# Gated cross-attention and routed experts: output projection as three fp32r products, and a new order of work in the tiles

## Chip, cores, metric

The kernel runs on one core of one Trainium2 chip. The metric is the device time of one launch in microseconds (us); the numbers below are medians of several launches. The engines of the core are TensorE (in the profile PE, its weight loads PEld), VectorE (DVE), ScalarE (ACT), GpSimd (POOL) and SyncE (SP, here only a DMA queue). Each works through its own instructions in the order in which they are written, and waits at semaphores for the others.

## What is computed

The reference, cut to what matters (2 x 1024 tokens of 256 numbers, 16 heads of 16, 77 context rows per batch, 8 experts with 1024 hidden units, of which each token takes the one with the largest router probability):

```
x = x + tanh(g_xattn) * attention(layernorm(x), ctx)      # Q, K, V, softmax over 77 keys, out @ wo.T + bo
x = x + tanh(g_ffn) * experts(layernorm(x))               # router = softmax(xt @ Wr + br)
# experts: h = relu(xn @ W1[idx] + b1[idx]); y = (h @ W2[idx] + b2[idx]) * gate
```

All inputs and the output are float32. The part that the change touches is `out @ wo.T` and what stands around it.

## The kernel before

The 2048 rows are cut into NT = 16 tiles of 128 rows. The launch has three stages: a start (weights transposed, K and V of the context prepared), the tile stage (attention, residual, layer norm and router for each tile; each tile's rows, their normalized form and their gate are stored to a scratch array in memory), and the expert stage (slots of 128 rows that share an expert are gathered from the scratch array, go through the two expert layers and are scattered to the output).

In the tile stage the loop `for n in range(NT)` stands once in the block of each engine, and round n of it mixes work on several tiles, written out by hand:

- TensorE in round n: `scores(n)` into pS; `transpose_O(n-2)`, which transposes the attention output On into the two halves of bank pA; `transpose_P(n-1, 0)`; `project(n-2)`, the output projection of tile n-2 into bank pB; the rest of the transposes of the probabilities of tile n-1 and of the next x (the latter into pA); `attend(n-1)`, the probabilities times V, into pB again; `query(n+1)`; `route(n)`, the router's product.
- ScalarE in round n: `copy_OT(n-2)` (pA into the SBUF tile OT, the stationary operand of the projection), `copy_PT(n-1, 0)`, `exp(n, 0)`, `copy_PT(n-1, 1)`, `copy_XX(n+1)`, `copy_PT(n-1, 2)`, `exp(n, 1)`, `query(n+1)` (the two copies of Q with its bias), `z_row(n-3)` and `x2_row(n-2)` (they write the row to be stored into one of three buffers `pay`; before tile i's they wait that the store of row i-3 has landed), `gate_exp(n-3)`.
- VectorE in round n: `smax(n, 0)` (row maxima of half the scores), `ssub(n, 0)` (their subtraction), `resid(n-2)` (projection in pB plus x; it frees pB for `attend(n-1)`), `smax(n, 1)`, `ssub(n, 1)`, layer norm statistics of two tiles, the router of tile n-3, the normalized x of tile n+2, and `norm(n-1)` in three steps (clamp of the softmax denominators into rden, reciprocal, product into On). Small steps of generators (`next(...)`) stand between the large ones.
- GpSimd in round n: `rstd2(n-2)` and `rstd1(n+3)` (powers for the layer norms), x plus bias, `store_row(n-4)` (the DMA to the scratch array), in some rounds steps of an expert-bias split.
- SyncE's queue: the weights of the last three experts (6, 7, 5) go into areas that the tile stage has used; each of these six loads of 1 MB is started when `x2_row` has counted one tile further (act_px2).

After round 15 follows a tail, written out for the tiles y = 14 and z = 15: on TensorE `transpose_O`, `project` and `attend` for them with the counts and ranks of the router between them, on VectorE the tables for the first slots (`rank`, `first_table`, `first_slots`), the first gather indices idxg and scatter indices idxs, `resid(y)`, `norm(z)`, `resid(z)`. Then the first slot begins with `transpose_z(0)` (again into pA) and `hidden(0, 0)`.

The projection of a tile is two matmuls in float32, one for each half of the 256 rows of the weight `wT["wo"]` (tile woT, 264 columns: 256 outputs and 8 router columns), at line 1647. In a trace each float32 matmul has two records. `OT` is written by ScalarE at line 623 and `xs` by VectorE at line 940. A float32 matmul by another way stands already in the expert stage: the second layer splits its hidden values and its weights in a high part rounded to fp32r and a low part, the rest, and adds three fp32r products (lines 1925 and 1930).

## Time and profile before

| | us |
|---|---|
| median of 3 runs | 278.69 |
| lowest, highest | 278.66, 279.93 |
| the profiled execution | 280.71 |
| its span in the trace | 278.8 |
| TensorE busy in it (matmuls) | 270.6 |
| VectorE, ScalarE, GpSimd busy | 202.9, 166.2, 135.8 |

The profile is of one execution. Its span runs from the first instruction to the last; the launch takes 1.9 us more than that. Times in the trace are counted from the start of the span. The tile stage lies between about 18 and 137 us, the expert stage behind it. A row of the trace that says `[0.17 <-DVE On L933]` means that the engine stood idle for 0.17 us before it, and that VectorE's instruction of line 933, which writes On, released it.

### The profile page before, as it was taken

Reading aid. Unit: us, or ns where it says so; the run is one execution under the profiler, and the core shown is the slowest. Engines: PE = TensorE matmul, PEld = TensorE weight load, DVE = VectorE, ACT = ScalarE, POOL = GpSimd, SP = SyncE. Lnnn points to the kernel's source line nnn. Section 1 sums busy time; section 2 is a strip of 40 time slices with the busy share of each in tenths; the row PEclk is TensorE's granted clock in tenths of the full one; section 3 lists DMA queues with packets and bytes.
Section 4 is the critical chain, followed back from the end, with each engine's and each line's share of the span. In section 5 each row is a group of like instructions: output and inputs, shape, how many; then the busy total and the mean of one; then the engine's idle time right before and its main releaser. Section 6 shows DMA issues by size and latency. Waiting matters only on the chain.

```text
span 278.8 us, 7269 instructions
## 1 busy us (share of the span) xinstructions
PE 270.6 (97%) x2320; PEld 239.7 (86%) x2320; DVE 202.9 (73%) x687; ACT 166.2 (60%) x444; POOL 135.8 (49%) x259
## 2 busy tenths in 40 slices
PE   8999999999999999999999999999999999999993
PEld 4879899999899999997888989999878789988992
DVE  6698579888888888879869976995446537443564
ACT  2535467777677777776396665785438435453551
POOL 3444046777877778644778242642212242222422
PEclk9999799999999999999999999999999999999999
DMA  7999996000002464545323131412201111220212
GB/s 206 288 307 374 372 378 243 33 36 31 30 29 89 186 185 182 183 175 185 117 76 118 58 99 57 136 46 75 77 9 59 52 51 49 83 58 24 60 49 72
DMA packets 19693, 34.43 MB, mean 124 GB/s; under 512 B 2392, under 2 KB 14486, under 8 KB 19643
## 3 DMA queue, kind: packets, MB, share of 16 engines
q1 hardware_dynamic: 15369, 21.26, 23.1%
q0 software_dynamic: 4128, 12.49, 13.7%
q8 instruction: 25, 0.41, 0.6%
q14 instruction: 25, 0.20, 0.2%
q10 hardware_dynamic: 146, 0.07, 0.1%
HBM read 27.45 MB, written 6.75 MB: 123 GB/s over the span
## 4 chain that ended last, share of the span: by engine, by line
PE 87%; DVE 6%; DMA 4%; issue 2%; POOL 0%; DVEq 0%; ACT 0%; POOLq 0%
PE pS L1855 21%; PE pB L1629 12%; PE pB L1925 10%; PE pT L1542 7%; PE pB L1647 6%; PE pA L1542 5%; PE pB L1930 5%; PE pS L1585 4%; PE pA L1565 3%; PE pT L1565 3%; DMA zin<-rows_dram,idxg 3%; PE pT L1657 2%; DMA W2s<-in_ctx_dram 1%; DVE hA L1304 1%; PE pT L1880 1%
## 5 line engine op out<-in xcount | busy, mean ns | idle before, releaser
L1855 PE MATMUL pS<-znf,W1c 128*128 128x128 f32 x576 | 71.2, 277 | 0.2 <-issue 0.2
L1855 PEld LDWEIGHTS pS<-znf,W1c 128*128 128x128 f32 x576 | 67.1, 192 | 3.4 <-issue 2.9
L458 POOL DMA_INDIRECT out_dram<-yo,idxs x17 | 17.4, 1021 | 73.0 <-DVE yo L1335 61.9
L1629 PE MATMUL pB<-VB,PT 128*128 128x51 f32 (+1 forms) x320 | 39.0, 270 | 0.2 <-DVE xs L940 0.2
L1925 PE MATMUL pB<-W2p,hT 128*128 128x512 f32 x136 | 39.0, 408 | 0.0
L745 ACT ACTIVATE hA<-pS,b1s 128x128 f32<-128x128 f32 x72 | 20.5, 367 | 30.6 <-PE pS L1855 27.7
L1629 PEld LDWEIGHTS pB<-VB,PT 128*128 128x128 f32 (+1 forms) x320 | 38.1, 192 | 0.6 <-issue 0.6
L1304 DVE TENSOR_SCALAR hA<-pS,b1s 128x128 f32<-128x128 f32 x72 | 20.2, 342 | 18.6 <-PE pS L1855 15.2
L605 ACT ACTIVATE Pb<-Pb 128x616 f32<-128x616 f32 x32 | 23.0, 718 | 15.4 <-DVE Pb L914 15.4
L756 ACT ACTIVATE hT<-hA 128x512 fp32r<-128x512 f32 x36 | 23.0, 641 | 15.2 <-DVE hA L1304 15.1
L441 POOL DMA_INDIRECT zin<-rows_dram,idxg x21 | 22.7, 1082 | 11.4 <-issue 5.3
L1925 PEld LDWEIGHTS pB<-W2p,hT 128*128 128x128 f32 x136 | 23.0, 189 | 4.8 <-issue 1.7
L906 DVE TENSOR_REDUCE mx<-pS 128x8 f32<-128x616 f32 x32 | 25.3, 790 | 1.9 <-PE pS L1589 1.9
L914 DVE TENSOR_TENSOR Pb<-pS,mx 128x616 f32<-128x616 f32 x32 | 25.3, 792 | 1.0
L1542 PE MATMUL pT<-cst,Pb 128*128 128x128 f32 (+1 forms) x160 | 25.5, 277 | 0.0
L1311 DVE TENSOR_TENSOR hT<-hA,hT 128x512 fp32r<-128x512 f32 x36 | 24.3, 686 | 1.5 <-ACT hT L756 0.2
L1930 PEld LDWEIGHTS pB<-W2p,hT 128*128 128x128 f32 x136 | 20.7, 188 | 3.9 <-DVE hT L1311 0.8
L613 ACT ACTIVATE PT<-pT 128x512 f32<-128x512 f32 x32 | 19.0, 595 | 7.2 <-PE pT L1542 6.5
L1930 PE MATMUL pB<-W2p,hT 128*128 128x256 f32 x136 | 21.5, 280 | 0.4 <-DVE hT L1311 0.4
L1542 PEld LDWEIGHTS pT<-cst,Pb 128*128 128x128 f32 (+1 forms) x160 | 19.5, 142 | 2.2 <-issue 0.5
L1647 PE MATMUL pB<-woT,OT 128*128 128x264 f32 x64 | 19.3, 426 | 0.6
L395 POOL TENSOR_SCALAR mv<-mv 128x1 f32<-128x1 f32 x16 | 3.8, 236 | 27.6 <-DVE mv L949 27.4
(279 smaller groups left out, 531.0 us busy)
## 6 DMA issues: line engine op xcount, KB each, us to landing
W1s<-in_L_ffn_W_dram SPq DMA_DIRECT2D x8, 1024.0 KB, 10.2
W2s<-in_L_ffn_W_dram SPq DMA_DIRECT2D x8, 1024.0 KB, 11.2
rows_dram<-pay POOLq DMA_DIRECT2D x16, 260.0 KB, 2.6
xs<-in_x_dram SPq DMA_DIRECT2D x3, 512.0 KB, 5.8
W2s<-in_sel_dram SPq DMA_DIRECT2D x1, 385.0 KB
zin<-rows_dram,idxg POOLq DMA_INDIRECT x21, 3.7
out_dram<-yo,idxs POOLq DMA_INDIRECT x17
W1s<-in_L_xattn_wk_dram SPq DMA_DIRECT2D x1, 256.0 KB, 3.1
```

Of the source, the lines that this page charges most:

```text
L605: e.activation(p2, p2, ACT.Exp, scale=0.25).then_inc(g["act_P"], 1)
L756: e.activation(hT[s % 2][0][:, 512 * n:512 * n + 512], half_of(s, n)[:, :], ACT.Copy).then_inc(g["act_hT"], 1)
L906: e.tensor_reduce(mx[:, i % 2, 8 * m:8 * m + 8].rearrange("p (n h) -> p n h", n=2), heads(m), AX.X, ALU.max).then_inc(g["dve_own"], 1)
L914: e.tensor_tensor(Pb[i % 2][:, 616 * m:616 * m + 616].rearrange("p (n h k) -> p n h k", n=2, h=4), heads(m), mx[:, i % 2, 8 * m:8 * m + 8] ...
L1304: e.tensor_scalar(half_of(s, 1)[:, 128 * c:128 * c + 128], pS[:, 2 * (s % 2) + 1, 128 * c:128 * c + 128], b1s[:, 4 + c, s:s + 1], 0.0, ALU ...
L1311: e.tensor_tensor(lo, half_of(s, n)[:, :], hi, ALU.subtract).then_inc(g["dve_hT"], 1)
L1542: return e.transpose(o, i, ident[0:n, 0:n])
L1629: t = e.matmul(pB[:, 17 * h0:17 * h0 + 51], PT[i % 2][0:n, c, :], VB[0:n, b, c, :], start=(c == 0), stop=(c == NC - 1), skip_group_check=True)
L1647: t = e.matmul(pB[:, 0:DX], OT[:, k, :], wT["wo"][:, k, :], start=(k == 0), stop=(k == 1))
L1855: t = e.matmul(pS[:, 2 * (s % 2) + n, 128 * c:128 * c + 128], W1c[k][n][:, 128 * c:128 * c + 128], znf[s % 2][:, 128 * k:128 * k + 128], s ...
L1925: e.matmul(o2, hT[s % 2][0][:, 128 * c:128 * c + 128], W2p[c // 2][:, :, D * (c % 2):D * (c % 2) + D], start=False, stop=True, skip_group_ ...
L1930: t = e.matmul(o, hT[s % 2][1][:, 128 * c:128 * c + 128], W2p[c // 2][:, 0, D * (c % 2):D * (c % 2) + D], start=False, stop=True, skip_gro ...
```

## The change

The projection's operands are split. ScalarE writes OT as fp32r (the rounded, high part); VectorE writes a new tile OT_low, pA minus OT, in `low_O(i)`. The weight is split once, in round 1 and 2: `wo_parts[:, 0]` by a copy on ScalarE, `wo_parts[:, 1]` by the subtraction `wo_low()` on VectorE. `project(i)` is then six fp32r matmuls: OT with both weight parts (four), then, after a wait for VectorE, OT_low with the high weight part (two). All that waited for OT to be copied because it wanted to write pA again now waits for VectorE's `dve_OT`.

In the tiles VectorE does `low_O` and `resid` ahead of `ssub(n, 0)`, with the first step of the next x's statistics between them. ScalarE's `exp(n, 0)` goes from between two `copy_PT` to where `exp(n, 1)` stood, `x2_row` and `z_row` come right behind it and ahead of `query(n+1)`, and `exp(n, 1)` comes last. Some tiles change their place in SBUF. One counter of semaphores (dve_idg2) is merged into another to make room for the new one.

```
-                exp(n, 0)
+                if n < 2:
+                    exp(n, 0)
...
-                    exp(n, 1)
+                    exp(n, 1 if n == 1 else 0)
+                if n == 2:
+                    e.wait_ge(g["dve_pois"], 1)
+                if n >= 2:
+                    x2_row(n - 2)
+                if n >= 3:
+                    z_row(n - 3)
...
                 if n >= 3:
-                    z_row(n - 3)
-                if n == 2:
-                    e.wait_ge(g["dve_pois"], 1)
+                    gate_exp(n - 3)
                 if n >= 2:
-                    x2_row(n - 2)
-                if n >= 3:
-                    gate_exp(n - 3)
+                    exp(n, 1)
...
+                    e.wait_ge(g["act_wT"], 5)
+                    e.activation(wo_parts[:, 0, :, :], wT["wo"][:, :, :], ACT.Copy).then_inc(g["act_wT"], 1)
...
+            def wo_low():
+                e.wait_ge(g["act_wT"], 7)
+                e.tensor_tensor(wo_parts[:, 1, :, :], wT["wo"][:, :, :], wo_parts[:, 0, :, :], ALU.subtract).then_inc(
+                    g["dve_wrc"], 1)
+
+            def low_O(i):
+                e.wait_ge(g["act_OT"], i + 1)
+                if i:
+                    e.wait_ge(g["pe_pr"], i)
+                e.tensor_tensor(OT_low[:, :, :].rearrange("p k n -> p (k n)"), pA[:, 0:256],
+                                OT[:, :, :].rearrange("p k n -> p (k n)"), ALU.subtract).then_inc(g["dve_OT"], 1)
...
+                if n == 2:
+                    wo_low()
+                if n >= 2:
+                    low_O(n - 2)
+                    next(x_stats, None)
+                    next(gated_row, None)
+                    resid(n - 2)
                 ssub(n, 0, t)
-                next(gated_row, None)
-                if n >= 2:
-                    resid(n - 2)
...
+            low_O(y)
             resid(y)
...
+            low_O(z)
             resid(z)
...
                 if i == 0:
-                    e.wait_ge(g["act_wT"], 5)
+                    e.wait_ge(g["dve_wrc"], 3)
+                for part in range(2):
+                    for k in range(2):
+                        e.matmul(pB[:, 0:DX], OT[:, k, :], wo_parts[:, part, k, :], start=(part == 0 and k == 0),
+                                 stop=False)
+                e.wait_ge(g["dve_OT"], i + 1)
                 for k in range(2):
-                    t = e.matmul(pB[:, 0:DX], OT[:, k, :], wT["wo"][:, k, :], start=(k == 0), stop=(k == 1))
+                    t = e.matmul(pB[:, 0:DX], OT_low[:, k, :], wo_parts[:, 0, k, :], start=False, stop=(k == 1))
```

The order that this gives. On VectorE, a round of the tile stage (from the first smax, line 906 before and 914 after, to the second ssub, 914 before and 922 after), first before, then after:

```order
109 L906 TENSOR_REDUCE mx<-pS 128x8
110 L991 RECIPROCAL Lg<-Lg 128x1
111 L914 TENSOR_TENSOR Pb<-pS,mx 128x616
112 L997 TENSOR_SCALAR pay<-Lg,tg 128x1
113 L940 TENSOR_TENSOR xs<-pB,xs 128x264
114 L906 TENSOR_REDUCE mx<-pS 128x8
115 L945 BN_STATS st<-xs 128x6
116 L914 TENSOR_TENSOR Pb<-pS,mx 128x616
117 L874 BN_STATS st<-xs 128x6
```

The same round after:

```order
135 L914 TENSOR_REDUCE mx<-pS 128x8
136 L1011 RECIPROCAL Lg<-Lg 128x1
137 L953 TENSOR_TENSOR OT_low<-pA,OT 128x256
138 L882 BN_STATS st<-xs 128x6
139 L1017 TENSOR_SCALAR pay<-Lg,tg 128x1
140 L960 TENSOR_TENSOR xs<-pB,xs 128x264
141 L922 TENSOR_TENSOR Pb<-pS,mx 128x616
142 L914 TENSOR_REDUCE mx<-pS 128x8
143 L965 BN_STATS st<-xs 128x6
144 L922 TENSOR_TENSOR Pb<-pS,mx 128x616
```

The new subtraction stands behind the first smax, the residual ahead of both ssub (Pb), and one of the statistics is drawn in between them.

On ScalarE, a round from `copy_OT` to the last instruction ahead of the next one, before:

```order
67 L623 ACTIVATE OT<-pA 128x256
68 L613 ACTIVATE PT<-pT 128x512
69 L605 ACTIVATE Pb<-Pb 128x616
70 L613 ACTIVATE PT<-pT 128x512
71 L586 ACTIVATE XX<-pA 128x256
72 L616 ACTIVATE PT<-pT 128x128
73 L617 ACTIVATE PT<-pT 80x128
74 L605 ACTIVATE Pb<-Pb 128x616
75 L599 ACTIVATE QT<-pA,bcol 128x128
76 L599 ACTIVATE QT<-pT,bcol 128x128
77 L641 ACTIVATE pay<-xs,mv 128x256
78 L634 ACTIVATE pay<-xs,pois 128x256
```

The same round after:

```order
66 L616 ACTIVATE PT<-pT 128x512 x2
67 L589 ACTIVATE XX<-pA 128x256
68 L619 ACTIVATE PT<-pT 128x128
69 L620 ACTIVATE PT<-pT 80x128
70 L608 ACTIVATE Pb<-Pb 128x616
71 L637 ACTIVATE pay<-xs,pois 128x256
72 L644 ACTIVATE pay<-xs,mv 128x256
73 L602 ACTIVATE QT<-pA,bcol 128x128
74 L602 ACTIVATE QT<-pT,bcol 128x128
75 L649 ACTIVATE Lg<-Lg 128x8
76 L608 ACTIVATE Pb<-Pb 128x616
```

Both row copies (pay) now stand ahead of both Q copies (QT), and the second exponential (Pb) stands last, right ahead of the next `copy_OT`.

In the tail, on VectorE, what stands behind the scatter indices idxs of the first slots, before:

```order
412 L1389 TENSOR_TENSOR idxs<-xh 128x4
413 L940 TENSOR_TENSOR xs<-pB,xs 128x264
```

and after:

```order
428 L1414 TENSOR_TENSOR idxs<-xh 128x4
429 L953 TENSOR_TENSOR OT_low<-pA,OT 128x256
```

The subtraction that the last projection waits for has the residual's old place, behind the tables and the routers.

## Rows read from the trace of the kernel before

**Rows 1.** Windows: stretch, length, busy us (count) of PE, PEld, DVE, ACT, POOL, clock, DMA share, GB/s.

```profile
88.23:95.32 7.09, 7.05 (x70) 6.44 (x67) 6.21 (x23) 5.37 (x15) 5.58 (x14) 1.00 0.46 187
31.00:32.00 1.00, 1.00 (x5) 0.79 (x4) 0.63 (x1) 0.69 (x2) 0.00 (x0) 0.50 1.01 395
```

**Rows 2.** Timeline, round 10: start, duration, engine, line, what, count, idle before.

```profile
88.36 0.79 DVE L906 TENSOR_REDUCE mx<-pS 128x8 f32<-128x616 f32 x1
...
88.70 0.38 ACT L623 ACTIVATE OT<-pA 128x256 f32<-128x256 f32 x1 [0.46 <-PE pA L1542]
...
89.14 1.16 PE L1647 MATMUL pB<-woT,OT 128*128 128x264 f32 x4
...
90.13 0.60 PE L1542 MATMUL pT<-cst,Pb 128*128 128x128 f32 x4
90.33 0.43 DVE L940 TENSOR_TENSOR xs<-pB,xs 128x264 f32<-128x264 f32 x1 [0.15 <-PE pB L1647]
...
93.89 0.37 ACT L599 ACTIVATE QT<-pT,bcol 128x128 f32<-128x128 f32 x1
...
94.27 0.17 DVE L923 TENSOR_SCALAR rden<-pB 128x16 f32<-128x16 f32 x1 [0.65 <-PE pB L1629]
...
94.57 0.81 PE L1585 MATMUL pS<-Kbd,QT 32*128 32x154 f32 x16
...
95.32 0.20 PEld L1542 LDWEIGHTS pA<-cst,On 128*128 128x128 f32 x2 [0.17 <-DVE On L933]
```

**Rows 3.** Timeline of PE in the expert stage: the products with fp32r operands.

```profile
187.62 0.63 PE L1930 MATMUL pB<-W2p,hT 128*128 128x256 f32 x4
188.09 1.09 PE L1925 MATMUL pB<-W2p,hT 128*128 128x512 f32 x4
```

**Rows 4.** Timeline, round 2; last, a page group: shape, count | busy us, mean ns | idle.

```profile
29.94 0.79 DVE L906 TENSOR_REDUCE mx<-pS 128x8 f32<-128x616 f32 x1
...
31.07 1.96 PE L1647 MATMUL pB<-woT,OT 128*128 128x264 f32 x4
...
L1311 DVE TENSOR_TENSOR hT<-hA,hT 128x512 fp32r<-128x512 f32 x36 | 24.3, 686 | 1.5 <-ACT hT L756 0.2
```

**Rows 5.** Timeline of DVE: round 3, and the last round, 15.

```profile
44.11 0.17 DVE L923 TENSOR_SCALAR rden<-pB 128x16 f32<-128x16 f32 x1
...
125.00 0.79 DVE L906 TENSOR_REDUCE mx<-pS 128x8 f32<-128x616 f32 x1
...
126.96 0.79 DVE L906 TENSOR_REDUCE mx<-pS 128x8 f32<-128x616 f32 x1
...
129.63 0.17 DVE L923 TENSOR_SCALAR rden<-pB 128x16 f32<-128x16 f32 x1 [0.26 <-PE pB L1629]
```

**Rows 6.** Timeline of the tail: residual of tile 14; projection and residual of tile 15.

```profile
132.79 0.43 DVE L940 TENSOR_TENSOR xs<-pB,xs 128x264 f32<-128x264 f32 x1 [0.42 <-PE pB L1647]
...
138.24 1.16 PE L1647 MATMUL pB<-woT,OT 128*128 128x264 f32 x4
...
140.29 0.16 DVE L1389 TENSOR_TENSOR idxs<-xh 128x4 int32<-128x4 f32 x1
140.40 0.43 DVE L940 TENSOR_TENSOR xs<-pB,xs 128x264 f32<-128x264 f32 x1
```

**Rows 7.** Timeline of the expert stage's start: the first gather that PE waits for.

```profile
159.78 1.01 POOL L441 DMA_INDIRECT zin<-rows_dram,idxg  x1 [2.77 <-DVE idxg L1484]
...
163.55 0.44 PE L1542 MATMUL pA<-cst,zin 128*128 128x128 f32 x2 [0.45 <-DMA zin<-rows_dram,idxg]
```

**Rows 8.** Round 9 and 10: a row's store, its time to landing, the row copy, a weight load.

```profile
88.14 0.37 SPq L321 DMA_DIRECT2D W1s<-in_L_ffn_W_dram  x1
89.95 0.65 POOL L422 DMA_DIRECT2D rows_dram<-pay  x1
DMA to landing us min/median/max: 4.3/4.3/4.3
94.64 0.49 ACT L634 ACTIVATE pay<-xs,pois 128x256 f32<-128x256 f32 x1
```

More of the change, by code:

```diff
@@ L112, in flamingo @@
         VB = sbt("VB", [128, B, NC, 51])
-        woT = sbt("woT", [128, 2, DX])
+        wo_parts = sbt("wo_parts", [128, 2, 2, DX], F32R)
+        OT_low = sbt("OT_low", [128, 2, 128], F32R)
         On = sbt("On", [128, D])
-        OT = sbt("OT", [128, 2, 128])
+        OT = sbt("OT", [128, 2, 128], F32R)
         mx = sbt("mx", [128, 2, H])
         rden = sbt("rden", [128, 2, H])
-        Pb1 = sbt("Pb1", [128, NC * 128])
+        sbt("below_PT1", [128, 496])
         PT1 = sbt("PT1", [128, NC, 128])
@@ L129, in flamingo @@
         st = sbt("st", [128, 4, 8])
-        sbt("below_W1c", [128, 2124])
+        Pb1 = sbt("Pb1", [128, NC * 128])
+        woT = sbt("woT", [128, 2, DX])
+        sbt("below_W1c", [128, 316])
         Pb = [sbt("Pb0", [128, NC * 128]), Pb1]
@@ L565, in _ @@
             used = e.value_load(slot_e[0:1, NS:NS + 1], min_val=FIRST, max_val=NS)
-            e.wait_ge(g["dve_idg2"], 1)
+            e.wait_ge(g["dve_ids2"], 2)
             for grp in range(2):
                 gather_small(grp)
-            e.wait_ge(g["dve_ids2"], 2)
+            e.wait_ge(g["dve_ids2"], 3)
             for s in range(KA - 1, FIRST):
@@ L1506, in _ @@
             e.wait_ge(g["dve_own"], t)
[L1507 removed]
+            e.tensor_tensor(idxg[:, NS:NS + 2], idt2, ids2[:, 0, :], ALU.add).then_inc(g["dve_ids2"], 1)
             e.wait_ge(g["dve_own"], t_e)
@@ L1637, in transpose_O @@
                 if i == NT - 1:
-                    e.wait_ge(g["act_OT"], NT - 1)
+                    e.wait_ge(g["dve_OT"], NT - 1)
                 transpose(pA[:, 0:128], On[:, 0:128])
@@ L1756, in _ @@
                     if n >= 2:
-                        e.wait_ge(g["act_OT"], n - 1)
+                        e.wait_ge(g["dve_OT"], n - 1)
                     else:
@@ L1862, in transpose_small_z @@
                 if grp == 0:
-                    e.wait_ge(g["dve_ids2"], 2)
+                    e.wait_ge(g["dve_ids2"], 3)
                     e.wait_ge(g["dve_b1"], 2)
```

5 lines of the change are left out of this document (2 added, 3 removed).

## The prediction

> **What bounds the kernel now.** I read the windows first, then the timeline of one round, then the rounds that differ from it. In a middle round TensorE is busy for 7.05 of 7.09 us [rows 1]; VectorE works 6.21 and ScalarE 5.37. The timeline of that round [rows 2] shows where TensorE still waits: its weight load for the projection starts 0.06 us after ScalarE has written OT (88.70 + 0.38 = 89.08, then 89.14), and its next transposes of On wait 0.17 us for VectorE (95.32). VectorE waits twice: 0.15 us for the projection ahead of the residual (90.33) and 0.65 us for attend ahead of rden (94.27). So TensorE sets the pace, but a loop through VectorE (attend, rden, On, transposes) lies right under it: whatever comes late to On is paid in full. The question is what the projection gives back per round, and where VectorE's new instruction stands in a wait of TensorE.
>
> **Part 1, the projection in a round.** Before: from the weight load at 89.14 the first matmul starts some 0.1 later (one load), and the next transposes start at 90.13 [rows 2]. That is four records of (90.13 - 89.24) / 4 = 0.222 us, 0.89 in all; a record is two passes of 264 columns at 0.111. After: six fp32r products. The expert stage shows their price: four of 256 columns take 188.09 - 187.62 = 0.47, so 0.117 each [rows 3], and 0.12 for 264 columns. The first four run from 89.24 to 89.72. The last two wait for OT_low. Its price is not in the trace. Nearest is the residual, 264 columns from PSUM and SBUF, 0.43 us [rows 2]; the fp32r subtraction of 512 columns in SBUF takes 0.69 [rows 4], half of that is 0.34. I take 0.42, with 0.34 to 0.5 as ends. It starts when smax is through (88.36 + 0.79 = 89.15) and OT is written (89.08), ends at 89.58, the weight load behind it starts at 89.64, and the matmuls at 89.75: two of them, until 89.99. That is 0.14 less than 90.13; with the ends 0.06 to 0.17. I take 0.12.
>
> The trace prices two passes at 0.222. The Trainium skill, "FP8 and Floating Point Precision", section Matmul Precision, says that true FP32 takes four passes through the array, while reduced FP32 reads the number once and truncates it; by that rule alone eight passes become six, and each round would give back 0.22, not 0.12. The rows agree with the count of passes; the difference is the weight load and the wait for OT_low, which the rule leaves out.
>
> **Part 2, VectorE's round.** It gets one instruction more (0.36 from start to start, as the residual has it: such instructions overlap by some 0.07), and part of it lies in the wait for the projection. Counted through: OT_low 89.15, statistics 89.50, gate 89.84, residual 90.21 (last product 89.87, plus 0.28 to its end as in [rows 3], where 0.63 is three steps of 0.117 and the last one's 0.28; plus 0.06 for the semaphore), first ssub 90.57, second smax 91.28, second ssub 92.3, and the rest of the round as before: VectorE is ready for rden at about 93.85. attend is through 0.12 earlier than before, at 94.15. So 0.3 us of the 0.65 are left, and the round holds at -0.12.
>
> Round 3 is another matter. There rden starts at 44.11 with no wait in front [rows 5], because the mask of the second batch is made in it. Counted the same way VectorE comes to rden at 44.37. TensorE would be ready for it at 43.98. So this round is 0.26 slower than before.
>
> **Part 3, ScalarE's round.** The two row copies (0.49 for the one at 94.64 [rows 8], the other somewhat longer) go ahead of the Q copies. The first exponential can start at about 91.8 and end at 92.45; the row copy from 92.4, the Q copies at 93.5 and 93.8; the second one ended at 93.89 + 0.37 = 94.26 before and scores started at 94.57 [rows 2]. There is room for about 0.4. It is used up by a wait that was hidden before: the row copy needs the landing of the store three rows back. A store issued at 89.95 landed 4.3 later, at 94.25, just ahead of the copy at 94.64 [rows 8]. That store was slow because a weight load of 1 MB had started at 88.14, let go by the row copy of the round before. With the copy 2 us earlier the load goes 2 us earlier too and is nearly over when the store is issued; I take 2.4 to 3 us to landing (an estimate between the 4.3 of this row and none of the load beside it). The store itself goes about 0.35 later (the statistics that GpSimd waits for are later). So the row copy starts at about 92.7 to 93.0 and scores at 94.3 to 94.6: no loss in rounds without a load, and most of the 0.12 gone in the rounds with one. I count rounds 4 to 9 with -0.12 (six, -0.7) and rounds 10 to 14 with -0.04 (five, -0.2).
>
> **Part 4, the first projection.** The split of the weight comes once. ScalarE's copy is hidden (it ends before OT(0)). VectorE's subtraction (528 columns, 0.69 as for 512 [rows 4]) starts behind smax, at 30.7, and OT_low behind it. Before, the four records ran from 31.07 [rows 4] at half clock (0.50 in that stretch [rows 1]), so at 0.44 each, until 32.83. After: weight load 31.4, four products of 0.22 from 31.6, two more, end 32.95. I count +0.15, with -0.1 to +0.6.
>
> **Part 5, the last round and the tail.** Here OT_low stands where VectorE is late already.
> - Round 15: VectorE starts its first smax at 125.00, behind steps of the router's ranks; the second smax is at 126.96, and rden at 129.63 after a wait of 0.26 [rows 5]. After: OT_low 125.71 to 126.13, products end 126.70, residual 126.76, ssub 127.11, second smax 127.82. That is 0.86 later, less the 0.26: On comes 0.6 later. TensorE waits for it. +0.6.
> - Tile 14: the residual at 132.79 waited 0.42 for the projection [rows 6], that is, tables kept VectorE until 132.37. OT_low(14) starts there, ends 132.79; two products, and the residual at 133.35. +0.55, also for TensorE, whose transposes stand behind the project.
> - Tile 15: TensorE starts the projection at 138.24, and VectorE has its residual at 140.40, right behind idxs at 140.29 [rows 6]. OT_low(15) takes that place: 140.40 to 140.83, products from 141.0, residual 141.46. VectorE is 1.06 later; TensorE, whose first slot starts behind the projection, 2.0. What of this is carried on? The first gather that TensorE waits for (0.45 at 163.55) was issued at 159.78, when VectorE had its indices [rows 7]. That chain is VectorE's and moves by 1.06, and TensorE's extra 0.9 goes into this wait and one at the first slot. +1.06.
>
> **The sum.** +0.15 + 0.26 - 0.7 - 0.2 + 0.6 + 0.55 + 1.06 = +1.7 us. Against the span: 278.8 to 280.5, and the profiled execution 280.71 (1.9 around the span) to 282.4. That execution lies 2.0 above the median of the runs, 278.69; the difference applied to the median gives 280.4.
>
> **Rivals.**
> - *All of the passes are won.* If OT_low is ready when the fourth product ends, a round gives 0.17 to 0.22: twelve rounds -2.3. For it: VectorE has slack in the rounds. Against: the count in part 1. With the other terms +2.6 it comes to 279.0, not slower than before. It decides if OT_low is done before 89.6 on the clock of round 10. The skill's count of passes would lead here.
> - *The row copy waits for its store.* If stores still take 4.3 us, the copy starts at 94.6, ScalarE's Q copies some 1.6 later than now, and scores 1.5 late once in two rounds: 0.6 a round, in rounds 10 to 14 +3, in all 283.4. For it: [rows 8]. Against: the load that made the store slow moves with the copy. It decides from 3 us to landing on.
> - *The clock stays low, or falls again.* It is at half, 1.2 GHz, in round 2, in a stretch where TensorE was busy throughout [rows 1], so it can be low without an idle engine. After the change TensorE stands idle for 0.5 us there, and for 2 us at tile 15. For it: these gaps. Against: rounds with gaps of 0.1 to 0.2 us ran at 1.00 [rows 1]. A further stretch of 3 us at half clock does work of 1.6 us less: 280.4 + 1.6 = 282.0. It decides if the granted clock is 0.5 past 33 or past 139.
> - *Faster.* Full gain of 0.22 in twelve rounds (-2.6), and the tail's delays (2.2) fully absorbed by gathers: 278.69 - 2.6 + 0.4 = 276.5. It needs that VectorE's chain of the tail is not what the gather waits for; [rows 7] names just that.
>
> **How the numbers follow.** A measurement of this kernel can tell about 0.5% from no change, 1.4 us: faster is under 277.3, slower over 280.1. Forecast as summed 0.48, all passes won 0.18, row copy 0.13, clock 0.12, faster 0.09. About a third of the forecast's own spread (279.6 to 281.2, from the ends of the price of OT_low and of part 4) lies below 280.1. Slower: 0.32 + 0.13 + 0.12 = 0.57; same: 0.16 + 0.18 = 0.34; faster 0.09. The likeliest is 280.4. The range 278.2 to 283.0 leaves out most of the faster case and the upper part of the row copy's.
>
> **What would show it.** In a middle round, project to next transposes 0.85 instead of 0.99 us, and a round of 6.98; VectorE's wait at rden about 0.3. In round 3 TensorE waits for On 0.5. Behind tile 15's fourth product about 2 us of idle time on TensorE, released by OT_low. Wrong would be: rounds of 7.1 or more with ScalarE waiting for a store; half clock behind 139; or a gather at 163.55 that has not moved.

## The result and the profile after

The changed kernel is slower. Its four executions took 284.34, 285.95, 287.63 and 288.63 us, median 286.79; beside them the kernel before took 278.77 (278.66 to 279.93). The ratio is 1.0218, interval 1.0128 to 1.0307. In a later set of runs it was 286.76 against 280.5: 1.0179, interval 1.0130 to 1.0227. Both intervals are clear of 1; both hold 1.02, so whether it is more than 2% is open. Ratios and intervals, here and below, leave out executions more than 1.5% above the fastest of their kernel; the medians do not. The forecast was 280.4, with a range up to 283.0. The sign was right, the size was not.

Two engines' lines of the page of after, the granted clock in 40 slices, and the chain that ended last:

```profile
PE 270.2 (96%) x2352; PEld 241.5 (85%) x2352; DVE 208.1 (74%) x704; ACT 164.6 (58%) x445; POOL 135.8 (48%) x259
...
PEclk9999799999999999999889999999999999999999
...
PE 69%; DVE 14%; issue 5%; DMA 5%; POOL 3%; ACT 3%; ACTq 0%; DVEq 0%; POOLq 0%
...
PE pS L1886 19%; PE pB L1956 10%; PE pB L1655 7%; PE pT L1568 5%; PE pB L1961 5%; PE pA L1568 4%; PE pB L1674 3%; DVE Pb L922 3%; PE pS L1611 3%; DMA rows_dram<-pay 2%; PE pA L1591 2%; PE pB L1678 2%; DVE mx L914 2%; PE pT L1591 2%; DMA zin<-rows_dram,idxg 1%
```

The store of a row (DMA rows_dram<-pay) holds 2% of the chain, and the clock has a second dip in the middle of the span. The profiled execution is the fastest of the four (284.34, span 282.5, against 278.8 before), so its trace explains 3.7 us; the other three have lower mean clocks (0.974 to 0.980, against 0.988), and I come to them below.

**A steady round does what was forecast.** TensorE in round 9, and the scores of round 10; timeline (start, duration, engine, line, what, idle before):

```profile
82.40 0.75 PE L1674 MATMUL pB<-wo_parts,OT 128*128 128x264 f32 x4
82.99 0.41 PE L1678 MATMUL pB<-wo_parts,OT_low 128*128 128x264 f32 x2
83.24 0.60 PE L1568 MATMUL pT<-cst,Pb 128*128 128x128 f32 x4
...
87.17 0.57 PE L1688 MATMUL pT<-wrc,XX 128*128 128x8 f32 x4
89.08 0.81 PE L1611 MATMUL pS<-Kbd,QT 32*128 32x154 f32 x16 [1.33 <-ACT QT L602]
```

From projection to next transposes it is 83.24 - 82.40 = 0.84 us; in [rows 2] it was 0.99. But at 89.08 the scores wait 1.33 us for QT. ScalarE shows why, and the second and third line show how long the store issued at 83.61 took to land:

```profile
87.52 0.51 ACT L637 ACTIVATE pay<-xs,pois 128x256 f32<-128x256 f32 x1 [1.85 <-DMA rows_dram<-pay]
...
L425 POOL DMA_DIRECT2D rows_dram<-pay x1: 662/662/662, 83.6 to 83.6; - x1
...
DMA to landing us min/median/max: 3.8/3.8/3.8
```

The row copy waits 1.85 us for its store, and both Q copies stand behind it. The windows of that time (columns as in [rows 1]) show that no load was beside it:

```profile
84.50:85.00 0.50, 0.50 (x7) 0.50 (x6) 0.50 (x2) 0.50 (x4) 0.41 (x2) 1.00 0.47 158
85.00:85.50 0.50, 0.50 (x7) 0.50 (x6) 0.50 (x2) 0.50 (x2) 0.48 (x1) 1.00 0.93 366
85.50:86.00 0.50, 0.50 (x6) 0.50 (x6) 0.50 (x2) 0.17 (x1) 0.40 (x1) 1.00 0.04 8
86.00:86.50 0.50, 0.50 (x6) 0.50 (x6) 0.50 (x4) 0.00 (x0) 0.00 (x0) 1.00 0.06 17
...
88.12 0.37 SPq L324 DMA_DIRECT2D W1s<-in_L_ffn_W_dram  x1
```

Most of the store moved by 85.7, at up to 366 GB/s; it landed at 83.61 + 3.8 = 87.4, and the weight load was issued only at 88.12, by the copy that had waited.

The trace also shows what held the landing up. Between its issue and its landing one packet of another queue moved; of the queues from 82 to 88 us (packets, MB, share of the engines' time), the first is the store's:

```profile
q0 software_dynamic: 80, 0.27, 11.6%
q8 instruction: 1, 0.02, 1.2%
```

The queue that the profile calls "instruction" moved 16 KB from 84.93 to 86.10, in the middle of the store. The store is 64 packets of 4 KB and 16 of 4 bytes, so four and one for each of the 16 DMA engines. Sixty of the 64 were through at 85.7; the last four, one engine's share, started one after another from 86.10 on, as soon as the 16 KB were through, and ended at 86.9. All 18 traces, of before, after and e1 to e16, agree. They record 118 landings of row stores that had no weight load beside them. All twenty of 3 us or more had such a 16 KB packet that began 0.8 to 2.0 us after the issue, and none that had no packet of an instruction queue took over 2.5. In the kernel before this packet moved at 85.70, behind the store of 82.86, which landed in 2.4. This is read from traces; no run moved that packet alone.

**The clock falls a second time.** The first stretch at half clock is that of [rows 1]; the second was not there before:

```profile
31.00:32.00 1.00, 0.57 (x4) 0.20 (x2) 1.00 (x3) 0.53 (x2) 0.00 (x0) 0.50 0.98 361
...
139.00:140.00 1.00, 1.00 (x35) 0.83 (x32) 0.79 (x4) 0.00 (x0) 0.76 (x1) 0.77 0.25 96
140.00:141.00 1.00, 1.00 (x4) 0.42 (x3) 0.93 (x9) 0.00 (x0) 0.76 (x3) 0.50 0.04 8
141.00:142.00 1.00, 1.00 (x5) 0.47 (x3) 0.86 (x5) 0.38 (x1) 0.99 (x2) 0.50 0.82 250
142.00:143.00 1.00, 1.00 (x6) 0.94 (x4) 0.89 (x6) 0.22 (x2) 0.74 (x3) 0.52 0.07 25
```

**The places where VectorE is late.** The first projection, the ends of rounds 3 and 15, the two tiles of the tail, and the gather of [rows 7]:

```profile
31.95 1.22 PE L1674 MATMUL pB<-wo_parts,OT 128*128 128x264 f32 x4 [0.43 <-DVE wo_parts L946]
...
46.13 0.20 PEld L1568 LDWEIGHTS pA<-cst,On 128*128 128x128 f32 x2 [0.61 <-DVE On L941]
...
133.16 0.20 PEld L1568 LDWEIGHTS pA<-cst,On 128*128 128x128 f32 x2 [0.69 <-DVE On L941]
...
135.20 0.52 PE L1678 MATMUL pB<-wo_parts,OT_low 128*128 128x264 f32 x2 [0.36 <-DVE OT_low L953]
...
143.33 0.42 DVE L953 TENSOR_TENSOR OT_low<-pA,OT 128x256 fp32r<-128x256 f32 x1
143.81 0.51 PE L1678 MATMUL pB<-wo_parts,OT_low 128*128 128x264 f32 x2 [0.59 <-DVE OT_low L953]
...
167.01 0.44 PE L1568 MATMUL pA<-cst,zin 128*128 128x128 f32 x2 [0.49 <-DMA zin<-rows_dram,idxg]
```

The gather has moved from 163.55 [rows 7] to 167.01, 3.46 us, which is nearly all of the 3.7.

### The profile page after: what moved, and what is told of

The parts are those of the page before. It is cut to its first block, busy times and chain, and to the rows that moved or that the text cites. A ratio compares the mean times of both kernels' runs of the same rounds, so it can differ in the third digit from the quotient of the medians.

```text
span 282.5 us, 7366 instructions
## 1 busy us (share of the span) xinstructions
PE 270.2 (96%) x2352; PEld 241.5 (85%) x2352; DVE 208.1 (74%) x704; ACT 164.6 (58%) x445; POOL 135.8 (48%) x259
## 4 chain that ended last, share of the span: by engine, by line
PE 69%; DVE 14%; issue 5%; DMA 5%; POOL 3%; ACT 3%; ACTq 0%; DVEq 0%; POOLq 0%
PE pS L1886 19%; PE pB L1956 10%; PE pB L1655 7%; PE pT L1568 5%; PE pB L1961 5%; PE pA L1568 4%; PE pB L1674 3%; DVE Pb L922 3%; PE pS L1611 3%; DMA rows_dram<-pay 2%; PE pA L1591 2%; PE pB L1678 2%; DVE mx L914 2%; PE pT L1591 2%; DMA zin<-rows_dram,idxg 1%
## 5 line engine op out<-in xcount | busy, mean ns | idle before, releaser
L731 ACT ACTIVATE znf<-pA,bcol 128x128 f32<-128x128 f32 x38 | 15.6, 476 | 0.8 <-PE pA L1568 0.8
```

## The experiments

All are medians of the executions of one set, with the ratio to the kernel before in the same set. "Clock" is the median of the executions' mean granted clock. "Less clock" is the median of time minus (1 - clock) x span, that is, the time with the half-clock stretches counted at half of their length. It is only a guide: where TensorE waits for something else, a slow stretch costs less than that (e15 and e16 below differ by 0.7 us in their medians, and this measure puts 1.9 of theirs on the clock).

| kernel | n | median us | ratio (95%) | clock | less clock |
|---|---|---|---|---|---|
| before (four sets) | 19, 27, 29, 35 | 280.5, 280.2, 280.5, 281.1 | 1 | 0.993 | 278.4 to 278.9 |
| changed | 4 | 286.79 | 1.0218 (1.0128 to 1.0307) | 0.977 | 280.6 |
| e12, changed again | 6 | 286.76 | 1.0179 (1.0130 to 1.0227) | 0.977 | 280.2 |
| e1, orders only | 10 | 282.73 | 1.0071 (1.0029 to 1.0113) | 0.989 | 279.2 |
| e2, products only | 10 | 281.0 | 1.0031 (0.9994 to 1.0068) | 0.985 | 277.3 |
| e3, ScalarE's old order | 4 | 294.41 | 1.0511 (1.0440 to 1.0582) | 0.980 | 288.9 |
| e4, OT_low early | 4 | 287.64 | none | 0.974 | 280.0 |
| e5, filled tail | 6 | 287.06 | 1.0230 (1.0190 to 1.0271) | 0.980 | 280.5 |
| e6, e2 + OT_low early | 12 | 280.13 | 0.9983 (0.9953 to 1.0013) | 0.994 | 276.9 |
| e7, x2 copy behind query | 9 | 282.94 | 1.0075 (1.0044 to 1.0106) | 0.984 | 278.3 |
| e8, e7 + OT_low early | 12 | 280.5 | 1.0020 (0.9990 to 1.0049) | 0.993 | 277.8 |
| e9, before, filled start | 12 | 279.89 | 0.9989 (0.9953 to 1.0024) | 0.999 | 279.7 |
| e10, e7 + filled tail | 14 | 283.37 | 1.0069 (1.0038 to 1.0101) | 0.988 | 279.9 |
| e11, e6 + wo in two steps | 12 | 279.69 | 0.9964 (0.9936 to 0.9992) | 0.988 | 276.9 |
| e13, e11 + filled start | 12 | 279.45 | 0.9957 (0.9921 to 0.9993) | 0.994 | 278.4 |
| e14, changed, all mends | 12 | 280.39 | 0.9985 (0.9951 to 1.0019) | 0.994 | 279.3 |
| e15, e9 + idle 2.3 us | 12 | 282.76 | 1.0059 (1.0019 to 1.0098) | 0.988 | 278.9 |
| e16, e9 + the same, filled | 12 | 282.02 | 1.0039 (1.0004 to 1.0075) | 0.996 | 280.1 |

### The parts of the change, one by one

e1 is the kernel before with both new orders and its own float32 projection:

```diff
 # VectorE, round n
-ssub(n, 0, t); next(gated_row, None)
-if n >= 2: resid(n - 2)
+if n >= 2: next(x_stats, None); next(gated_row, None); resid(n - 2)
+ssub(n, 0, t)
 # ScalarE: exp(n, 0), x2_row, z_row ahead of query(n + 1); exp(n, 1) behind it
```

> The kernel before with the new order alone (residual ahead of the first subtraction on VectorE, both exponentials and the two row copies in their new places on ScalarE); the projection is the float32 one. Two theories. Waits: of the 8 us of the change about 1.7 come from row copies that now wait for the store three rows back in the middle of ScalarE's round (1.2 + 0.3 + 0.15 us in rounds 9, 11 and 13), and this is their place: 280.5 to 281.5 us, with waits of ScalarE's row copy for the store again. Clock: most of the 8 us are further stretches at half clock (3.4 us long, 1.7 us of loss each), let loose by gaps of TensorE at the products' waits for OT_low; those are missing here, so the mean clock stays near that of before (0.994 or more), and this kernel is within 2 us of before. If the order itself lets the clock fall: 284 or more.

It was 0.7% slower. Its middle rounds are 7.09 us, those of before: the order alone gives nothing. The row copy waited up to 2.47 us for its store, with the float32 projection as well, and round 3 took 7.53 (7.10 before, 6.95 in e2 below). So these costs belong to the order, not to the products.

e2 has the products and neither order; low_O stands right behind the first smax:

```diff
 t = smax(n, 0)
+if n >= 2: low_O(n - 2)
 ssub(n, 0, t)
 next(gated_row, None)
 if n >= 2: resid(n - 2)
```

> The fp32r products alone, with both engines' order as before (OT_low right behind the first smax, subtraction, then residual). Waits: rounds at 6.98 instead of 7.09 us (-1.3 over twelve), first projection +0.7, round 3 +0.3, last round and tail +2.2, no wait of the row copies: 280.5 to 281. Clock: the gaps at the first projection and at tile 15 are still there, so the mean clock lies at 0.974 to 0.988 as in the changed kernel, and the time at 283 to 286.

Its middle rounds take 7.02 us, 0.07 less than before, and no row copy waits more than 0.5. The ratio, 1.0031, cannot be told from 1. Its clock is 0.985, and by the last column the gain goes there. The last projection of its tail:

```profile
139.51 0.51 PE L1675 MATMUL pB<-wo_parts,OT_low 128*128 128x264 f32 x2 [1.84 <-DVE OT_low L950]
...
141.00:142.00 1.00, 1.00 (x5) 0.55 (x3) 0.93 (x7) 1.00 (x4) 0.57 (x3) 0.50 0.78 166
```

TensorE waits 1.84 us for OT_low, and 1.5 us later the granted clock is 0.50.

e3 is the changed kernel with the ScalarE order of before:

> The changed kernel with ScalarE's order of before (exponential 0 between two copies, row copies behind Q's). Both theories: no wait of the row copy for its store, so rounds 9, 11 and 13 lose nothing: 1.7 us less than the changed kernel, 284.5 to 285.5, if the mean clock stays at 0.974 to 0.988. If the row copies' waits are what the clock hangs on, the clock comes back to 0.99 and the time to 281 or 282.

Every theory missed this. A round takes 7.90 us, 0.93 more than in the changed kernel. One round of e3, ScalarE and TensorE:

```profile
97.15 0.72 ACT L608 ACTIVATE Pb<-Pb 128x616 f32<-128x616 f32 x1 [1.61 <-DVE Pb L919]
97.77 0.58 ACT L616 ACTIVATE PT<-pT 128x512 f32<-128x512 f32 x1
...
98.40 1.09 PE L1652 MATMUL pB<-VB,PT 128*128 128x51 f32 x8 [0.76 <-ACT PT L616]
```

With the residual ahead of it, the first ssub is written 1 us later, ScalarE's exponential waits for it, and the second copy of PT, which TensorE needs for attend, stands behind that exponential. So the two orders belong together: whoever moves the residual forward on VectorE must move the exponential back on ScalarE.

### OT_low in the tail

e4 changes only the tail of the changed kernel, e6 makes the same edit on e2:

```diff
-together(islice(early, 5), islice(table, 5)); low_O(y)
+together(islice(early, 3), islice(table, 3)); low_O(y)
+together(islice(early, 2), islice(table, 2))
...
 together(router(y - 1))
+low_O(z)
...
-low_O(z)
 resid(z)
```

> The changed kernel with OT_low of tiles 14 and 15 made as soon as OT is there (in between the tables of tile 14, behind the router of tile 13), no other edit. Waits: TensorE's gaps of 0.6 us at tile 14 and 1.5 to 2 us at tile 15 go, VectorE's chain to the indices of the fifth slot is 0.5 + 0.6 us shorter: 285.5. Clock: with the gap behind tile 15 gone at least one half-clock stretch goes with it (1.7 us more): 283.5 or less, mean clock 0.98 or more in every run.

> The three products with both orders of before (as in e2), and in the tail the subtraction that makes OT_low ahead of the work that delayed it: for tile 14 after three pieces of the tables rather than five, for tile 15 ahead of the index arithmetic. In the profile of e2 project(15) waited 1.84 us and project(14) 0.41 us for it. Theory W: 2 us less than e2 when the clock is the same, so a time less the clock's share ((1 - mean clock) x span) of 274.5 to 275.5 against 276.6 in e2 and 278.5 before. Theory C adds: without the 1.84 us wait the stretch at half clock at 141 us goes in part of the executions, and the median is 276.5 to 278.5. If the wait only passes to the next item (gathered rows), 280 to 281.

Four executions of e4, from 282.38 to 292.01, settle nothing: its profile has row copies that wait 2.34 and 2.15 us, a stretch at half clock behind the second, and another from 140.2 on, in the tail, with no idle time of TensorE of 0.2 us or more in the 10 us ahead of it. On e2 the edit is clean. The last projection no longer waits, the window that stood at 0.50 in e2 is at 1.00, and the median clock goes from 0.985 to 0.994:

```profile
136.54 0.76 PE L1672 MATMUL pB<-wo_parts,OT 128*128 128x264 f32 x4
137.27 0.51 PE L1676 MATMUL pB<-wo_parts,OT_low 128*128 128x264 f32 x2
...
141.00:142.00 1.00, 0.88 (x8) 0.69 (x8) 0.95 (x6) 1.00 (x3) 1.00 (x2) 1.00 0.77 162
```

The ratio fell from 1.0031 to 0.9983 only, with intervals that overlap. Less the clock, the two are 277.3 and 276.9, not the 2 apart that I expected; the waits of 2.2 us that went were probably covered in part already.

### The row copy

e7 moves one instruction of the changed kernel; e8 has e4's edit too:

```diff
 if n >= 3: z_row(n - 3)
-if n >= 2: x2_row(n - 2)      # stood ahead of z_row
 if n + 1 < NT: query(n + 1)
+if n >= 2: x2_row(n - 2)
 if n >= 3: gate_exp(n - 3)
```

> The changed kernel, except that ScalarE copies a row's x part (x2_row, the copy that waits for the store of three tiles before) behind the evacuation of the next query and not ahead of it; z_row stays ahead. Theory W (the copy's wait for its store delays QT, the scores and the round: 1.2, 0.5 and 0.15 us in the rounds that end at 89.82, 104.17 and 118.96 us of the profile): all rounds 4 to 11 take 6.95 to 7.55 us and the time less the clock's share is 1.5 to 2 us under that of the changed kernel (280.6), so 278.7 to 279.1; the median about 283 to 285, as the clock decides. If the row copy's wait cost nothing by itself (the rounds were long for the clock or the scores' own inputs), the rounds stay at 8.3 and 7.4 us and the time at 286 to 287.

> The edits of e7 and the early OT_low in the tail (as in e4) together on the changed kernel. The sum of the parts, by waits: 280.6 less 1.8 (rows) less about 1 (OT_low at tiles 14 and 15) = 277.8 less the clock's share, which would be 279.5 to 282 on the clock of 0.994 to 0.985. Against e6 it tells whether the new order of both engines is worth its 0.08 us a round (6.95 against 7.02) once the row copy no longer waits: the new order costs 0.29 us in round 3 and the late OT wait of the first projection 0.5 us more, so e6 is expected to stay 1 to 3 us ahead.

```profile
86.64 0.37 ACT L602 ACTIVATE QT<-pT,bcol 128x128 f32<-128x128 f32 x1
87.50 0.51 ACT L637 ACTIVATE pay<-xs,pois 128x256 f32<-128x256 f32 x1 [0.49 <-DMA rows_dram<-pay]
...
87.33 0.81 PE L1611 MATMUL pS<-Kbd,QT 32*128 32x154 f32 x16
...
89.12 0.75 PE L1674 MATMUL pB<-wo_parts,OT 128*128 128x264 f32 x4 [0.18 <-ACT OT L626]
```

The store still lands late (4.2 us in this profile), the copy still waits for it, and the scores no longer wait for the copy: rounds 9 and 11 take 6.94 and 6.93 us, not 8.33 and 7.42. The wait is not free in its new place either. The second exponential and the next OT stand behind the copy, so the projection of round 10 waits 0.18 us for OT and that round takes 7.08; at the same store the projection waits 0.40 us in e8 and 0.75 in e14, whose rounds take 7.31 and 7.66. The ratio falls from 1.022 and 1.018 to 1.0075, 3 to 4 us for one moved instruction, of which 1.9 are in the rounds of the profile. e8 takes another half per cent away (the two intervals just touch), and its clock is 0.993 against 0.984 in e7, whose last projection waited 1.84 us. e6 and e8 came out closer than I expected, 0.4% apart, with intervals that overlap.

### Why the clock falls

e9 is the kernel before with three matmuls, results unread, ahead of the first router matmuls; e5 and e10 have six such matmuls at the end of the tile stage, in the changed kernel and in e7:

```diff
 # e9, round 1
+e.wait_ge(g["dve_Sm"], 4); warm(3, pS[:, 3, :])
 route(0)
 # e5 and e10
-project(y)
+project(y, 2, pS[:, 2, :])    # two between the fourth product and the fifth
+warm(2, pS[:, 3, :])
 counts(0)
-project(z)
+project(z, 2, pS[:, 3, :])
```

> The changed kernel with TensorE's gaps at the end of the tile stage filled: two matmuls of onesb (512 columns, 0.22 us each, their results read by nobody) between the fourth and the fifth product of project(14), two of them ahead of the counts of table entries, and two between the fourth and the fifth product of project(15). Theory C (the second stretch at a granted clock of 0.50, 139.7 to 142.9 us, comes from the waits and the tiny matmuls ahead of it): the stretch is gone in most executions, the mean clock of a run goes from 0.974 to 0.988 up to 0.986 to 0.994, and the median falls by 1.5 to 3 us, to 284 or less. Theory W (only waits count, the clock is by chance): no shorter stretch, and 0.4 us more for the two matmuls ahead of the counts: 287.

> The kernel before, with three matmuls of onesb (512 columns, 0.22 us each at the full clock, results unread) put ahead of the first router matmuls, among the 2.4 us of 8-column matmuls that stand right before the stretch at a granted clock of 0.50 at 29.8 to 33.0 us. Theory C (the stretch comes from how little TensorE's columns do there): the stretch is gone in most executions, the mean clock of a run is 0.998 to 1.0 rather than 0.992 to 0.994, and the time that of before's undisturbed executions, 278.4 to 278.9, plus 0.65 us: 279.0 to 279.6 against a median of 280.2 to 280.5. If the fall comes for another reason: clock 0.993 as before and 280.9 to 281.2.

> e7 with e5's six matmuls in TensorE's gaps at the end of the tile stage; OT_low is as late as in the changed kernel. e7 ran at a mean clock of 0.984 in seven of nine executions, and its profile has a second half-clock stretch at 142.8 to 146. Theory C: the filled gaps keep the clock there, mean clock 0.992 to 0.994, 1.7 us less and 0.4 us more for the pair ahead of the counts, so 281 to 282 against 282.9. If it is the length of the tiny count matmuls or where the stretch falls by chance: clock 0.984, 283.3.

e9 gives a clear answer on the clock. In the kernel before TensorE was not idle ahead of the first stretch, which begins at 29.5; it ran 8-column matmuls from 26.59 on:

```profile
26.59 1.06 PE L1786 MATMUL pT<-wrc,W1s 128*128 128x8 f32 x8
...
27.95 1.04 PE L1657 MATMUL pT<-wrc,XX 128*128 128x8 f32 x8
...
28.00:29.00 1.00, 1.00 (x13) 0.98 (x13) 0.00 (x0) 0.00 (x0) 0.36 (x1) 1.00 1.12 355
```

In e9:

```profile
26.62 0.59 PE L1789 MATMUL pT<-wrc,bcol 128*128 128x8 f32 x4
27.06 0.81 PE L1537 MATMUL pS<-onesb 128*128 128x512 bf16 x3
27.71 0.95 PE L1657 MATMUL pT<-wrc,XX 128*128 128x8 f32 x8
...
30.00:31.00 1.00, 0.96 (x5) 0.68 (x4) 0.90 (x2) 0.79 (x2) 0.00 (x0) 1.00 1.09 410
```

The window is at 1.00, and round 2 takes 7.09 us rather than 8.34. Eight of twelve executions had a mean clock of 0.998 or more; of the 110 of before in all sets, 16 did. Their median is 278.9 us, that of the 88 with one stretch (0.990 to 0.994) 280.7. That is what goes with one stretch: 1.8 us. The time of e9 itself cannot be told from that of before (0.9989, 0.9953 to 1.0024); the three matmuls take 0.65 us themselves.

e5 and e10 did not bring the time down, against what I wrote. e5's profile has no stretch in the tail, but one from 89.5 on, behind scores that had waited for the row copy:

```profile
87.78 0.81 PE L1611 MATMUL pS<-Kbd,QT 32*128 32x154 f32 x16 [1.79 <-ACT QT L602]
...
90.00:91.00 1.00, 1.00 (x6) 1.00 (x6) 0.30 (x2) 0.03 (x1) 0.94 (x2) 0.50 1.06 438
```

e10 has a higher clock than e7 (0.988 against 0.984) and the same time. Its profiled execution was at half clock from 28.9 to 46.0 and says nothing of the tail. So I made the delay itself, on e9:

```diff
 warm(WARM[4], pS[:, 3, :])       # e15; e16: WARM[4] + 9
+e.wait_ge(g["dve_idxs"], 1)
 project(z)
```

> e9 (the kernel before with the filled start, mean clock 1.0 in eight of twelve executions, 279.9 us), with one wait more: the projection of tile 15 waits until VectorE has written idxs, so TensorE stands still for about 2.2 us there (as it did for 1.84 us in e2), with before's float32 projection. Theory C: the idle time itself lets the granted clock fall right behind it, a stretch of 3.4 us at 0.50 at 139 to 143 us, mean clock lower by 0.006, and the time 279.9 + 2.2 + 1.7 = 283.8. Theory W: idle time costs its length alone, 282.1, with the clock at 1.0.

> The same as e15, but nine more filling matmuls (512 columns, 0.22 us each, 2 us) stand ahead of that wait, so that TensorE is busy for nearly all of the time for which it stood still in e15. Theory C: no second stretch, clock as in e9, 279.9 + 2.2 = 282.1, 1.7 us under e15. Theory W, and any theory in which the clock falls there for the tiny count matmuls ahead of it: the same time and clock as e15.

e15 first, then e16:

```profile
139.73 1.16 PE L1647 MATMUL pB<-woT,OT 128*128 128x264 f32 x4 [2.30 <-DVE idxs L1389]
...
142.00:143.00 1.00, 1.00 (x4) 0.52 (x3) 0.90 (x8) 1.00 (x4) 0.71 (x3) 0.50 0.80 183
```

```profile
136.01 2.54 PE L1537 MATMUL pS<-onesb 128*128 128x512 bf16 x11
138.91 1.16 PE L1647 MATMUL pB<-woT,OT 128*128 128x264 f32 x4 [0.36 <-DVE idxs L1389]
...
142.00:143.00 1.00, 1.00 (x11) 1.00 (x10) 0.93 (x8) 1.00 (x4) 1.00 (x2) 1.00 0.36 146
```

The idle 2.30 us are followed by a stretch at half clock, the filled ones are not. One of twelve executions of e15 had a clock of 0.994 or more, eight of twelve of e16. That the idle time lowers the clock at this place is shown. The delay itself, filled, cost 1.4 us by the ratios (0.9989 in e9, 1.0039 in e16). The price of the lower clock was 0.7 us in the medians (282.76 and 282.02, with intervals that overlap), less than the 1.7 expected, probably since what stands behind it in the expert stage waits for gathers anyway.

### The mends together, and the changed kernel again

```diff
 # e11 (and e13, e14): wo_parts in two steps
 query(2)
+e.activation(wo_parts[:, 0, :, 0:D], wT["wo"][:, :, 0:D], ACT.Copy)
...
-e.activation(wo_parts[:, 0, :, :], wT["wo"][:, :, :], ACT.Copy)
+e.activation(wo_parts[:, 0, :, D:DX], wT["wo"][:, :, D:DX], ACT.Copy)
 # VectorE: wo_low(0, D) at the end of round 1, wo_low(D, DX) behind smax(2, 0)
```

> e6 (three products, both orders of before, OT_low early in the tail), with wo_parts made in two steps: its 256 columns right after the copy of woT, while ScalarE and VectorE wait for the wo times Wr product (2.0 and 2.2 us in e6's profile), and only the last 8 columns behind it. In e6 round 2 took 8.61 us against 8.34 before, and wo_low (0.70 us) stands ahead of the first score subtraction. Expected: round 2 shorter by 0.4 to 0.7 us, the median 0.4 to 0.7 under e6's (280.1, so 279.4 to 279.8) by waits alone. If that stretch is bound by TensorE at the half clock and not by the preparation, no change.

> e11 (three products, old orders, OT_low early in the tail, wo_parts in two steps) with the three filling matmuls of e9 ahead of the first router matmuls. e9 took the first half-clock stretch away in 8 of 12 executions and was 0.6 us faster by the median. Theory C: the same here, mean clock 0.998 to 1.0, the median 0.3 to 0.8 us under e11's (279.7 there, 0.9964 of before), so a ratio of 0.993 to 0.996. If round 2 of e11 (7.57 us) is already bound by something else, ratio 0.996 to 0.999.

> The changed kernel with everything that the runs pointed to: x2_row behind the query, OT_low early in the tail, wo_parts in two steps, three filling matmuls at the start. e8 (without the last two) was at 1.002 of before. Theory: 0.7 us less by the split, 0.6 by the filling: ratio 0.997 to 0.999; and 0.5 to 1.5 us behind e13, since rounds 3 and 12 are 0.3 us longer each with the new order and round 14 0.36 longer, against 0.08 us less in each of the others. If the new order is worth what it was to bring, it is ahead of e13.

> The changed kernel, unaltered, beside the others on this chip, for its spread: by waits 280.6 (its four runs less the clock's share), by clock 0.974 to 0.988. If theory W plus C holds, the time follows the mean clock: 284.3 where it is 0.988, 286 at 0.98, 288 at 0.974; and the profile again has the row copy's waits of 1 us and more in the rounds that follow the stores at 83.6, 97 and 112 us.

In e11 the large subtraction lies in VectorE's wait for the 8-column products, and what is left behind the first smax is small:

```profile
26.47 1.23 DVE L945 TENSOR_TENSOR wo_parts<-woT,wo_parts 128x512 fp32r<-128x512 f32 x1 [0.17 <-ACT wo_parts L701]
...
29.92 0.17 DVE L945 TENSOR_TENSOR wo_parts<-woT,wo_parts 128x16 fp32r<-128x16 f32 x1
```

Round 2 takes 7.57 us (8.61 in e6), and e11 and e13 are ahead of before by 0.4%, intervals that just leave out 1. They cannot be told apart: only four of twelve executions of e13 ran without a stretch, so the filling works less well there than in e9. e14, with the new orders, is 0.3% behind e13, inside the intervals: from the start of round 3 to the start of the tail it takes 92.92 us, e13 91.82, before 92.65. e12 repeats the result, with row copies that wait 2.20 and 0.76 us and again a stretch at half clock behind the first of them. The store that this copy waited for was another one, issued at 68.53; here the 16 KB packet fell into it (from 69.8 on), and it landed in 4.2 us, while that of round 9 landed in 2.4.

## Why the prediction was wrong

The shifts below are differences of the starts of On's transposes in the two profiles, after less before.

| part | forecast us | measured us |
|---|---|---|
| up to round 2 | 0 | +0.39 |
| round 2, first projection | +0.15 | +0.29 |
| round 3 | +0.26 | +0.28 |
| rounds 4 to 8 | -0.60 | -0.61 |
| round 9 | -0.12 | +1.24 |
| rounds 10 to 14 | -0.20 | +0.36 |
| round 15 | +0.60 | +0.50 |
| tile 14 | +0.55 | +1.11 |
| tile 15 to the gather of [rows 7] | +1.06 | -0.10 |
| the rest | 0 | +0.24 |
| span | +1.7 | +3.7 |

**Part 1 held.** Projection to transposes 0.84 us (forecast 0.85), OT_low 0.41 to 0.42 (0.42), middle rounds 6.93 to 6.97 (6.98), before 7.09. The Trainium skill's count of passes ("FP8 and Floating Point Precision", section Matmul Precision) would have given 0.22 a round; measured were 0.12 to 0.16.

**Part 2 held.** VectorE's wait at rden is 0.20 us (forecast 0.3, before 0.65), and round 3 came 0.28 longer, with TensorE waiting 0.61 for On.

**Part 3 is the step that failed.** It put the slow landing of [rows 8] down to the weight load beside the store, took 2.4 to 3 us for the others, and counted "no loss in rounds without a load". Of the loads that was right. In the kernel before, the stores with a load beside them landed in 4.3, 3.9, 4.1 and 5.1 us, those without in 2.4 (61.04, 68.13, 82.86, 132.40); in the trace of after, those with one landed in 3.0, 2.4, 3.1 and 2.6 (90.55, 105.82, 113.24, 127.68), near the estimate. The loss came in round 9, which has no load: the store at 83.61 landed in 3.8 us, the row copy waited 1.85 for it, and the round came 1.24 later instead of 0.12 earlier. What held this store up was the 16 KB packet of the instruction queue. In the tile stage of before no such packet fell into a store without a load, so the rows could not tell of it; that e7 and e8 have such a store too (4.2 and 4.4 us) and lose 0.14 and 0.37 us in their round, where the changed kernel loses 1.4, shows that the place of the copy sets most of the price. The cost was in the list as a rival: "It decides from 3 us to landing on". That rival got 0.13, and it happened in another shape: 1.24 us at once in round 9, where no load is, and in rounds 10 to 14, where it had put 3 us, only 0.32 and 0.15 (rounds 11 and 13). The Trainium skill, "DMA: Bandwidth & Descriptors", section Anatomy of one DMA, says that the semaphore's update waits until the last byte is confirmed in the target memory; this trace agrees: the last packet of that store ended at 86.9 and the landing is at 87.4, and of the store at 69.13, which landed in 2.4 us, the two are 71.2 and 71.6.

**Part 4 was low by 0.14** (0.29, in its range of -0.1 to +0.6); e11 shows what it could have been, whose split took round 2 from 8.61 us (e6) to 7.57.

**Part 5 held in its waits and missed what they lead to.** Round 15 came 0.50 later (forecast 0.60). At tile 14 TensorE waited 0.36 (0.55); the 1.11 of the table hold also the 1.4 us at half clock between 139.5 and the transposes at 140.95. At tile 15 TensorE waited 0.59, not 2, because at half clock it came to the projection late (142.06). e2, e7 and e12, which came there at full clock, waited 1.84, close to the 2.0 of the forecast. The forecast carried +1.06 on to the gather; summed over both tiles it was 1.01 (1.11 - 0.10), of 1.61.

**The rivals were treated as if one excluded the other.** "The clock stays low, or falls again" had 0.12 and a price of 1.6, once. The sum let waits cost their length only. The runs show that they are linked: the row copy's wait and the wait for OT_low leave TensorE idle. Between 25 and 150 us it was idle for 1.6 us or more in nine places of all profiles. In eight of them the clock was at half within 1.8 us of the end of that idle time (e1, e2, e5, e7 and e15 once, e12 twice, e4 at 89.0); in e4 an idle 1.82 us at 71.1 was not followed by one. There is none in the tails of e6 and e16, where the wait was gone or filled. In the other three executions of the changed kernel the mean clock was 0.974 to 0.980: (1 - 0.974) x 286 is 7.4 us of such loss, against 2 in the kernel before. Less clock, the changed kernel is 2 us over before, close to the +1.7 of the sum, though by other terms; by this measure, which is a guide only, the other 4 to 5 us of the median go with the clock.

The experiments give the parts without that measure. The changed kernel stands at 1.022 and 1.018 of before, with the row copy behind the query at 1.0075 (e7; the forecast was 280.4 to 278.69, 1.0061), and with OT_low early in the tail as well at 1.0020 (e8). So the row copy's place was worth 1.0 to 1.4%, waits and the clock behind them together, where part 3 had nothing. OT_low's place in the tail was worth about half a per cent, near what part 5 had for the two tiles (+1.61 us).

Not settled: why the stretch comes in some executions and not in others of the same kernel, and four stretches that came in the tail with no idle time of 0.8 us or more ahead of them: at 139.5 in the profile of after, 140.2 in e4, 135.3 in e14 and 141.6 in e3. The first three begin within the run of 8- and 32-column count matmuls, with TensorE busy there (windows at 1.00). Such matmuls did it at the start of the kernel (e9); for the tail this was not shown, since e5 and e10 changed other things too, and the kernel before has the same matmuls (from 135.91 on) and no fall.

**The base was another error.** 278.69 was the median of three executions. In its four later sets, 110 executions, the kernel before has medians from 280.2 to 281.1, since most have one stretch at half clock. The profiled one, 280.71, was the ordinary case. The 2.0 us that I took off rest on two of the three, 278.66 and 278.69, whose times are those of executions without a stretch; their clocks are not on record.

## What to carry to other kernels

An instruction that waits for a DMA does not belong ahead of one that the busiest engine needs: its landing varies from run to run and row to row (2.4 to 6.0 us here), also by packets that no line of the kernel issues, and moving one row copy behind the query was worth 1.0 to 1.4%. When a change opens a gap on a TensorE that is busy 99% of the time, price the gap and the clock that may fall behind it together. And when a new instruction is put behind what an engine does at its busiest, in the last rounds or in a tail, give it the place by who waits for it: with the same work, earlier places for OT_low in the tail took the ratio from 1.0031 to 0.9983 (e2, e6) and from 1.0075 to 1.0020 (e7, e8), each pair hardly clear of noise alone, both the same way.

## What the runs showed of the hardware

- Eight-column matmuls that keep TensorE busy by the profile (1.00 of each window) still come before a fall of the granted clock to 0.50; with three matmuls of 512 columns among them (0.65 us) eight of twelve executions had no such fall (e9), against 16 of 110 in the kernel before.
- Idle time of TensorE of 1.6 to 2.3 us went with a half-clock stretch in eight of nine places; an idle 1.33 us (after, at 87.75) and 1.52 us (e14, at 140.6) did not. With matmuls whose results nobody reads in its place, the same delay left the clock at 1.00 (e16).
- A store of 260 KB moved within about 1 us and landed 2.4 to 2.5 us after its issue with nothing beside it, and 3.4 to 4.7 us after it where a 16 KB packet of the instruction queue fell into its middle in the tile stage (after, e1, e4, e5, e7, e8, e10, e12, e14, e15). In the store of 83.61 four of its 64 packets, one engine's share, moved only behind that packet, and the landing came 0.5 us behind the last of them.
- The fp32r subtraction of the weights took 1.23 us for 512 columns in e11 (at 26.47), and 0.70 for 528 in the changed kernel (at 31.11). In e11 a TENSOR_TENSOR of GpSimd (0.72 us, from 26.43) ran beside it, in e13 and e14 too (1.24 and 1.25 us); in the changed kernel GpSimd was idle there. No run tests whether that is the cause.
